# Cross-attention kernel: x scaled in turned form from group 2 on, constant products in the ramp, gain of two groups on VectorE

## The reference

```
# layer 0, once for s = a (ctx_512) and once for s = v (fside)
x1n = ln(x) * g1_s + b1_s ; x2n = ln(s) * g2_s + b2_s
q, k, v = x1n @ Wq_s + bq_s, x2n @ Wk_s + bk_s, x2n @ Wv_s + bv_s
out_s = softmax(q @ k.T * E**-0.5) @ v @ Wo_s + bo_s
res = out_a + out_v + x
y = (ln(res) * g + b) @ fc_W + fc_b + res
# layer 1
Q, K, V = y @ Wq + bq, ctx_512 @ Wk + bk, ctx_512 @ Wv + bv
result = y + softmax(Q @ K.T * E**-0.5) @ V @ Wo + bo
```

## Time and profile before

| | us |
|---|---|
| median of 3 executions | 154.44 |
| lowest and highest | 153.74 and 155.4 |
| the profiled execution, its time | 154.15 |
| the profiled execution, span of its instructions | 152.1 |
| TensorE busy | 144.1, 95% of the span |
| VectorE busy | 119.7, 79% |
| ScalarE busy | 117.0, 77% |
| GpSimd busy | 83.7, 55% |

### The profile page before, as it was taken

How to read it: one execution, slowest core, us unless ns; L and a number is a source line. 1 busy time by engine, 2 the same in 40 slices (tenths; PEclk the granted TensorE clock), 3 DMA queues, 4 the chain that set the end, 5 groups by cost and what they waited for, 6 DMA issues and landing times.

```text
span 152.1 us, 6148 instructions
## 1 busy us (share of the span) xinstructions
PE 144.1 (95%) x2320; PEld 104.1 (68%) x2320; DVE 119.7 (79%) x351; ACT 117.0 (77%) x410; POOL 83.7 (55%) x112
## 2 busy tenths in 40 slices
PE   5999999799999999999999999999999999999771
PEld 5987767688566766656866767657874877766440
DVE  1557999968899979899889757988677799668733
ACT  3436778568989788967977999787996878796970
POOL 2566999679438861878177575595674141201220
PEclk9999999999999999999999999999999999999998
DMA  5995799570770608786445019707300402201215
GB/s 154 346 386 179 227 312 370 142 274 3 238 241 15 211 8 263 237 232 186 165 144 173 4 43 244 248 8 249 135 4 0 142 2 73 73 0 69 75 71 207
DMA packets 13449, 23.40 MB, mean 154 GB/s; under 512 B 1660, under 2 KB 4332, under 8 KB 13420
## 3 DMA queue, kind: packets, MB, share of 16 engines
q1 hardware_dynamic: 12988, 22.61, 45.6%
q10 hardware_dynamic: 432, 0.41, 0.8%
HBM read 18.69 MB, written 4.32 MB: 151 GB/s over the span
## 4 chain that ended last, share of the span: by engine, by line
PE 92%; ACT 3%; issue 2%; DVE 1%; POOL 0%; POOLq 0%; ACTq 0%
PE ps L1758 10%; PE ps L1740 10%; PE ps L1699 9%; PE ps L1773 6%; PE ps L1731 6%; PE ps L1709 6%; PE ps L1747 6%; PE ps L1766 5%; PE ps L1574 5%; PE ps L1808 5%; PE ps L1684 5%; PE ps L1719 5%; PE ps L1783 4%; PE ps L1800 3%; PE ps L1791 2%
## 5 line engine op out<-in xcount | busy, mean ns | idle before, releaser
L579 POOL TENSOR_TENSOR prob<-exp,rsum 128x512 f32<-128x512 f32 x16 | 16.7, 1044 | 23.6 <-DVE rsum L1231 23.4
L585 POOL TENSOR_TENSOR prob<-exp,rsum 128x256 f32<-128x256 f32 x16 | 9.8, 616 | 19.7 <-DVE rsum L1300 19.6
L539 POOL TENSOR_TENSOR cfv_sb<-cf_sb,rows 128x512 f32<-128x512 f32 x16 | 17.0, 1061 | 5.8 <-PE ps L1731 3.5
L844 ACT ACTIVATE exp<-ps,exp_bias 128x64 f32<-128x64 f32 x64 | 19.3, 322 | 1.0 <-DVE exp_bias L1295 0.9
L825 ACT ACTIVATE gain_sb<-ps,res_rstd 128x128 f32<-128x128 f32 x64 | 18.3, 372 | 1.6 <-PE ps L1758 1.2
L547 POOL TENSOR_TENSOR cfk_sb<-cfv_sb,rows 128x512 f32<-128x512 f32 x16 | 17.0, 1060 | 1.1 <-POOL rows L532 0.2
L1758 PEld LDWEIGHTS ps<-wd,resT_sb 128*128 128x128 f32 x128 | 15.8, 191 | 2.3 <-issue 1.9
L1758 PE MATMUL ps<-wd,resT_sb 128*128 128x130 f32 x128 | 17.3, 278 | 0.0
L1699 PE MATMUL ps<-zT_sb,m 128*128 128x512 f32 x32 | 17.0, 617 | 0.0
L1740 PE MATMUL ps<-mix_sb,w 128*128 128x512 f32 x32 | 16.8, 608 | 0.0
L555 POOL TENSOR_TENSOR zT_sb<-xt_sb,x_spread 128x512 f32<-128x512 f32 x12 | 15.2, 1278 | 2.7 <-DMA x_spread<-rows_dram 2.4
(11 more groups left out here) (148 smaller groups left out, 342.5 us busy)
## 6 DMA issues: line engine op xcount, KB each, us to landing
x_sb<-in_x SPq DMA_DIRECT2D x16, 256.0 KB, 3.8
xt_sb<-in_xt SPq DMA_DIRECT2D x16, 256.0 KB, 3.9
out<-out_sb SPq DMA_DIRECT2D x16, 256.0 KB, 2.2
cf_sb<-in_cf SPq DMA_DIRECT2D x15, 256.0 KB, 3.3
x_spread<-rows_dram SPq DMA_DIRECT2D x6, 512.0 KB, 4.7
ct_sb<-in_ct SPq DMA_DIRECT2D x16, 128.0 KB, 4.0
w_sb<-in_w SPq DMA_DIRECT2D x1, 448.0 KB, 4.5
cf_sb<-in_cf ACTq DMA_DIRECT2D x1, 256.0 KB, 4.5
```

The lines of the kernel that those rows point to most:

```text
L539: pool.tensor_tensor(cfv_sb[:, g % CFV_SLOTS, :, :, :], cf_sb[:, g % CF_SLOTS, :, :, :], wide_cf(cf_rstd, g), ALU.mult).then_inc(cfv_pool, 1)
L579: pool.tensor_tensor(prob0[:, g % PROB0_SLOTS, :, :, :], exp0[:, g % EXP0_SLOTS, :, :, :], wide0(rsum0, g), ALU.mult).then_inc(prob0_done, 1)
L844: last = nc.scalar.activation(exp1[:, g % EXP1_SLOTS, p, :], ps[:, bank + u, v * S:(v + 1) * S], ACT.Exp, bias=exp1_bias[:, g, p:p + 1], a ...
```

## The change

The groups that are scaled and then transposed are 0 and 1 in place of 0 to 3, and the way over DRAM begins with batch 2. The gain of groups 14 and 15 goes to VectorE (`early_gain`, which was there but unused), and the probabilities of group 15 in layer 1 are formed by VectorE (`late_probs1`). TensorE's first run of constant products has 6 in place of 13, one more follows between `fold_v` and `fold_a`, and eight stand in the ramp behind the folds, before `t0(0)`, `s0(0)`, `s0(1)` and `out0(0)`. The order on all five queues is written anew. The core of the diff:

```diff
-TURNED = [0, 1, 2, 3]
+TURNED = [0, 1]
-SPREAD_FROM = 3
+SPREAD_FROM = 2
-GAIN_ON_DVE = []
+GAIN_ON_DVE = [14, 15]
+PROB1_ON_DVE = [15]
...
+        def prob1_ready(eng, g):
+            ready(eng, g, PROB1_ON_DVE, prob1_dve, prob1_pool)
...
             load_x(0)
+            load_wk()
+            load_w128()
+            load_wt()
+            load_wv()
+            load_x(1)
             load_cf(1)
-            load_wk()
-            load_wv()
-            load_w128()
-            load_x(1)
+            load_x(2)
             load_cf(2)
             load_cf(3)
...
             load_cf(7)
-            load_xt(0)
+            store_rows(2)
+            load_xt(1)
+            load_cf(8)
             load_x(6)
-            load_xt(1)
             load_xt(2)
+            spread_x(2)
...
+            scale_cf(1)
             z(1)
-            scale_cf(1)
             shifts(1)
+            shifts(2)
             shift_cf(1)
-            z(2)
-            z(3)
             scale_cf(2)
-            shifts(2)
+            shift_cf(2)
             probs0(0)
-            shift_cf(2)
+            shifts(3)
             scale_cf(3)
+            probs0(1)
+            scale_cf(4)
+            scale_xt(2)
+            scale_xt(3)
             shift_cf(3)
...
+            def late_probs1(g):
+                dve.wait_ge(rsum1_done, g + 1)
+                need(dve, prob1T_made, g - PROB1_SLOTS + 1)
+                v.tensor_tensor(prob1[:, g % PROB1_SLOTS, :, :], exp1[:, g % EXP1_SLOTS, :, :],
+                                wide1(rsum1, g), ALU.mult).then_inc(prob1_dve, 1)
...
             pe.wait_ge(constants_made, 1)
-            keep_busy(13, 0)
+            keep_busy(6, 0)
             fold_v(0)
+            keep_busy(1, 6)
             fold_a(6)
-            keep_busy(3, 2)
-            zT(0, 2)
-            fold_bias(3)
-            keep_busy(1, 0, (wq_v_done, 1), (wk_v_done, 1))
+            fold_bias(2)
+            fold_am(3)
+            zT(0, 4)
+            fold_wv(5)
             fold_m0(0)
-            fold_wv(7)
+            keep_busy(1, 0, (m0_done, 1))
             t0(0, 0)
...
+            fold_fca(1)
+            cfT(0, 3)
+            keep_busy(3, 3, (cfT_copied, 1))
+            s0(0, 3)
+            fold_wfc(0)
+            zT(1, 7)
+            turn_rows(2, 1)
+            fold_w(0, (wfc_done, 1))
+            cfT(1, 1, (rowsT_copied, 1))
+            t0(1, 7)
+            keep_busy(3, 6, (t0_copied, 2))
+            s0(1, 6)
+            prob0T(0, 1)
+            fold_bq1(0, (out0_bias_done, 1))
+            cfT(2, 2)
+            mix0(0, 3)
+            turn_rows(3, 1)
+            keep_busy(1, 0, (bq1_done, 1))
+            out0(0, 0)
+            fold_t1b(7)
+            prob0T(1, 6)
+            resN(0, 0)
+            dense(0, 1, (cfT_copied, 3))
+            mix0(1, 3)
+            t0(2, 0, (res_stats_done, 1))
+            out0(1, 3)
+            x1T(0, 4)
+            t0(3, 7, (t1_bias_done, 1))
...
+            dense(14, 2, (bias_row_done, 14))
+            dense(15, 6, (x1T_done, 14), (mix1_copied, 12))
+            t1(13, 0, (exp1_done, 13))
+            x1T(14, 1)
+            prob1T(12, 2, (bias_row_done, 15))
+            s1(13, 3)
+            out1(11, 5, (bias_row_done, 16))
             t1(14, 0)
+            x1T(15, 7)
+            mix1(12, 1)
+            s1(14, 5, (final_done, 12))
+            t1(15, 7)
+            out1(12, 0)
+            s1(15, 2)
             prob1T(13, 4)
```

More of the change, by code:

```diff
@@ L1853, in _ @@
+            cfT(3, 7)
+            cfT(4, 1, (diff0_done, 3))
+            x1T(1, 2)
+            t0(4, 7, (cfT_copied, 4))
+            s0(3, 3, (bias_row_done, 2))
+            t1(1, 2)
+            cfT(5, 0, (rowsT_copied, 3))
+            prob1T(0, 7, (t0_copied, 5))
+            s1(1, 5)
+            s0(4, 3, (diff0_done, 4))
+            mix1(0, 1)
             prob0T(2, 7)
[L1854 to L1857 removed]
+            t0(5, 0, (cfT_copied, 6))
@@ new lines, in _ @@
+            x1T(2, 4, (res_stats_done, 4))
+            turn_rows(5, 7, (cfT_copied, 7))
+            prob0T(4, 6)
+            s0(6, 0, (bias_row_done, 3))
+            t1(2, 7, (rowsT_copied, 4))
+            prob0T(5, 4)
+            x1T(3, 5)
+            s1(2, 2, (bias_row_done, 4))
+            mix0(4, 6)
+            mix0(5, 0, (diff0_done, 7))
+            out1(1, 4, (x1T_done, 4))
+            out0(4, 6)
+            cfT(7, 0, (mix0_copied, 6))
+            t1(3, 1)
+            resN(4, 7)
@@ new lines, in _ @@
+            dense(4, 2, (exp1_done, 3))
+            out0(5, 0, (cfT_copied, 8))
+            t0(7, 1)
+            s1(3, 4, (final_done, 2))
+            x1T(4, 0, (res_done, 6))
+            prob0T(6, 6)
+            prob1T(2, 7)
+            resN(5, 1, (t0_copied, 8))
+            s0(7, 2, (bias_row_done, 5))
+            mix1(2, 6)
+            t1(4, 0)
+            t0(8, 1, (res_stats_done, 6))
+            s1(4, 6)
+            out1(2, 4)
+            mix0(6, 2, (diff0_done, 8))
+            dense(5, 0, (t0_copied, 9))
@@ new lines, in _ @@
+            cfT(8, 2, (mix0_copied, 7))
+            out0(6, 3)
+            cfT(9, 4, (final_done, 3))
+            t0(9, 5)
+            prob0T(7, 2, (cfT_copied, 9))
+            x1T(5, 0, (bias_row_done, 6))
+            resN(6, 7, (exp1_done, 5))
+            prob1T(3, 1)
+            s0(8, 2, (prob0T_copied, 8))
+            t1(5, 0)
+            mix1(3, 6, (res_stats_done, 7))
+            mix0(7, 4)
+            s1(5, 0)
+            s0(9, 2, (diff0_done, 9))
+            turn_rows(6, 7, (mix1_copied, 4))
@@ new lines, in _ @@
+            x1T(7, 1)
+            mix0(8, 2)
+            s1(6, 4)
+            out1(5, 6, (prob0T_copied, 10))
+            t1(7, 0)
+            out0(8, 1)
+            mix0(9, 2)
+            s1(7, 6, (final_done, 6))
+            t0(10, 0)
+            prob1T(6, 5)
+            turn_rows(7, 2, (mix0_copied, 10))
+            out0(9, 3)
+            resN(8, 0, (t0_copied, 11))
+            mix1(6, 1, (rowsT_copied, 6))
+            s0(10, 4)
+            out1(6, 6)
+            dense(8, 0, (res_stats_done, 9))
@@ new lines, in _ @@
+            out0(10, 5)
+            t0(12, 2, (rowsT_copied, 7))
+            prob0T(11, 3, (mix1_copied, 8))
+            dense(10, 0, (exp1_done, 9))
+            cfT(13, 2, (t0_copied, 13))
+            resN(10, 7)
+            mix0(11, 3)
+            s0(12, 5)
+            t0(13, 7, (res_stats_done, 11))
+            prob1T(8, 2, (cfT_copied, 14))
+            out0(11, 3)
+            cfT(14, 4)
+            s1(9, 0, (bias_row_done, 11))
+            mix1(8, 6, (t0_copied, 14))
+            out1(7, 2, (res_done, 12))
@@ new lines, in _ @@
+            s0(13, 4, (cfT_copied, 15))
+            dense(11, 6, (mix1_copied, 9))
+            x1T(10, 3, (final_done, 8))
+            t0(14, 2)
+            resN(11, 0, (exp1_done, 10))
+            prob0T(12, 1)
+            t1(10, 5, (diff0_done, 14))
+            s0(14, 2)
+            mix0(12, 0, (res_stats_done, 12))
+            cfT(15, 4)
+            t0(15, 5, (t1_copied, 11))
+            out1(8, 2, (diff0_done, 15))
+            prob0T(13, 0, (mix0_copied, 13))
+            x1T(11, 1)
```

1228 lines of the change are left out of this document (540 added, 688 removed).

## The result

| | median us | lowest to highest | runs |
|---|---|---|---|
| before | 154.09 | 153.29 to 155.4 | 4 |
| changed | 162.56 | 162.04 to 163.13 | 4 |

The ratio is 1.054 [1.046, 1.063]: the changed kernel is slower by 5.4%, and its time lies 5.6 us above the upper end of the range. The profiled execution took 162.04 us with a span of 160.2, 8.1 us more than before. The ratios of this document leave out executions that were over 1.5% longer than the fastest of their kernel, the medians do not, so that a median need not match its ratio.

The account below looks back on a forecast made before the run. TensorE's own work bounds the middle, a chain of short steps the tail; the change acts in ramp and tail. Terms -2.1, +0.4, +1.2, -0.9, waits 1.0 give -0.4; tail +0.1; total -0.3: median 154.1 us, eight-in-ten range 151.8 to 157.0.

Parts of the forecast that it names:

- the low clock: Ramp: TensorE's gap before fold_v may delay the clock's rise, at latest to t0(0); +0.4 us, bounds 0 and 0.75.
- Rival 2: Ramp: TensorE stays at the lower clock past t0(0), rising only behind s0(1); 157.3 us, chance 0.17.
- the likeliest case: Whole kernel: the prediction's own sum of terms, median 154.1 us, chance 0.48.
- Start of the folds: Ramp: shorter first run and earlier wk load let fold_v start at 5.15 in place of 7.24; -2.1 us.
- Constant products: Ramp behind fold_v: nine constant products in place of five, most on TensorE's path; +1.2 us.
- Transposes of x: Ramp: TensorE drops zT(2) and zT(3) for one more turn_rows; -0.9 us.
- New waits: Ramp: only two groups can start early, so TensorE has less to do while their chains run; 1.0 us.
- The hand trace: Ramp: new lists followed with late clock; s0(1) at 19.9, t0(2) at 27.3, out0(1) ends at 29.0.
- The path of x over DRAM: Ramp: rows of batch 2 land at 23.7, scale_xt(2) starts at 25.9; cost 0, 2.2 us to spare.
- Rival 3: Ramp: x_spread(2) lands late behind four loads, beyond the 2.2 us of cover; 156.4 us, chance 0.05.
- The tail: Last groups: gain and probabilities on VectorE save, out1(12) ahead of s1(15) costs 0.5; sum +0.1 us.
- Rival 1: Ramp: clock rises as early as before and the 1.0 us of waits are absent; 152.3 us, chance 0.30.

Follow-up runs that it names:

- a9: Changed kernel with 9 constant products in the first run in place of 6; 160.67 us, ratio 1.045 against the kernel before.
- b6: Kernel before with its first run of constant products cut from 13 to 6; 156.99 us, ratio 1.023 against the kernel before.
- a13: Changed kernel with its first run of constant products set back from 6 to 13; 156.0 us, ratio 1.016 against the kernel before.
- a13no8: Changed kernel with 13 products in the first run and without the eight in the ramp; 155.77 us, ratio 1.017 against the kernel before.
- a6no8: Changed kernel, still 6 products in the first run, without the eight in the ramp; 162.34 us, ratio 1.050 against the kernel before.
- bno5: Kernel before without the five constant products that stand behind the first 13; 151.32 us, ratio 0.982 against the kernel before.
- bno5p: bno5 with the layer 1 probabilities of group 15 on VectorE; 151.56 us, ratio 0.980 against the kernel before.
- an8z2: a13no8 with groups 2 and 3 scaled on GpSimd (early) and transposed on TensorE again; 159.13 us, ratio 1.016 against the kernel before.
- an8out1: a13no8 with s1(15) issued ahead of out1(12); 157.21 us, ratio 1.016 against the kernel before.
- an8tail: a13no8 with the gain of groups 14, 15 back on ScalarE and group 15's probabilities on GpSimd; 156.63 us, ratio 1.019 against the kernel before.

## Why the prediction was wrong

The failing step is **the low clock**, a term of +0.4 us with bounds of 0 and 0.75, and in two ways.

The first is when the clock rises. I let it rise by `t0(0)` at the latest and gave a later rise 0.17. It rose at about 22.4 us. Against a late rise I had written that from 5.15 to about 10 the engine has no long gap. This is true of the changed kernel (there is no wait between 5.51 and 14.1) and it did not help. Nor is an early rise enough: `a9` had the clock and lost it at the folds at about 9.4 us, `b6` had it at 6.26 and lost it at about 7.8. How much the length of the first run is worth, the ratios of `a13` and `b6` say: 3.8 and 2.3 points. Why the clock stays up or not over these folds is not shown.

The second is the price. The bound of 0.75 doubled only the matmuls of the folds, `zT(0)`, `fold_wv` and `fold_m0`, and not their latencies. The run that tells is `a13no8`, the changed list with the clock up. Its timeline of TensorE:

```profile
1.52 5.37 PE L1585 MATMUL ps<-ones,ident 128*128 128x128 f32 x26 [1.52 <-POOL ident L503]
6.73 0.39 PE L1588 MATMUL ps<-affine_v,wq_sb 128*128 128x129 f32 x2
...
9.36 0.61 PE L1688 MATMUL ps<-ident,z_sb 128*128 128x128 f32 x4
...
11.96 1.10 PE L1710 MATMUL ps<-zT_sb,m 128*128 128x512 f32 x2 [0.48 <-ACT m L715]
...
14.43 0.70 PE L1720 MATMUL ps<-cfT_sb,t_sb 64*64 64x64 f32 x32 [0.77 <-ACT cfT_sb L789]
...
19.62 0.69 PE L1720 MATMUL ps<-cfT_sb,t_sb 64*64 64x64 f32 x32 [0.87 <-ACT t_sb L794]
...
21.11 0.35 PE L1676 MATMUL ps<-biases,w_sb 128*128 128x1 f32 x2 [0.21 <-DVE out_bias L1156]
...
23.48 1.13 PE L1751 MATMUL ps<-mix_sb,w 128*128 128x512 f32 x2 [0.55 <-ACT mix_sb L820]
...
27.62 1.13 PE L1710 MATMUL ps<-zT_sb,m 128*128 128x512 f32 x2
28.59 1.02 PE L1751 MATMUL ps<-mix_sb,w 128*128 128x512 f32 x2
```

| stretch on TensorE | changed | `a13no8` | difference | `a6no8` |
|---|---|---|---|---|
| to `fold_v` | 5.51 | 6.73 | -1.22 | 5.69 |
| `fold_v` to `t0(0)` | 9.61 | 5.23 | +4.38 | 9.01 |
| `t0(0)` to `s0(0)` | 5.34 | 2.47 | +2.87 | 3.99 |
| `s0(0)` to `s0(1)` | 6.82 | 5.19 | +1.63 | 8.77 |
| `s0(1)` to `out0(1)` | 8.48 | 8.97 | -0.49 | 10.01 |
| `out0(1)` to the end | 124.4 | 124.7 | -0.3 | 125.1 |

The whole loss is in the second to fourth stretch, 8.9 us, with 1.2 given back by the earlier start and 0.8 behind `s0(1)`: 6.9 us of span, of which the ramp has all. The two kernels differ in the eight products too. In the changed kernel one of them stands in the second stretch and three each in the third and fourth, 0.59, 1.58 and 0.86 us from start to start, together 3.0 of the 8.9. `a6no8` has neither them nor the clock, and its column gives the low level alone, for as long as it lasted in that execution. Ahead of `t0(0)`, where my bound allowed 0.75, it costs 3.78 us (9.01 against 5.23): the folds stand one behind the other on TensorE, and the small ones, down to those of one column, grew nearly as much as the large (two pairs of one column from start to start 0.24 us in `a13no8`, 0.44 in the changed kernel). Without the wait of 0.48 us for `m`, which both have, the stretch is 1.8 times as long. Rival 2 had the mechanism right and the place nearly (a rise behind `s0(1)`; in the changed kernel it came between `s0(0)` and `s0(1)`), but took over this price for the folds and counted 3.2 us behind them, from `t0(0)` to `s0(1)`. There the changed kernel has 4.5 more than `a13no8`, and `a6no8`, where the clock did come up only behind `s0(1)`, has 5.1 more without a single product. So the likeliest case and the rival erred by the same row. By the rule that I quoted from the Trainium skill (TensorE: Matmul & The Clock Gate, What's actually happening) the sum was to take the later bound or more: the trace agrees with the more.

The other steps:

- **Start of the folds.** Forecast 5.15, measured 5.51 (-1.73 in place of -2.1); `fold_v` waited 1.06 us for `affine_v`. Right in kind, 0.4 off. The six products ended at 4.45, forecast 4.2, which cost nothing here.
- **Constant products.** +1.2 for four more. At either level of the clock the eight weigh nothing that can be told (0.1 and 0.4 points, where their forecast length of 2.1 us would be 1.4). That a product on TensorE's path costs its length held for the five in the profiles of `bno5` and `bno5p`, not for the eight. In `a13no8` TensorE waits ahead of `t0(0)`, `s0(0)` and `s0(1)`, the places where they stood, so I take them to have filled waiting time there.
- **Transposes of x.** -0.9. Not seen: `an8z2`, which takes them back, has the ratio of `a13no8`. But 0.9 us is 0.6 points, less than these intervals can tell.
- **New waits.** +1.0 was too small. In `a13no8` the waits for `m`, `cfT_sb`, `t_sb`, `out_bias` and `mix_sb` are 0.48, 0.77, 0.87, 0.21 and 0.55, 2.9 us, where TensorE had hardly waited before: from 10 to 26 us it was busy 15.81 us before and is 12.92 in `a13no8`. The first three, 2.1 us, stand ahead of `s0(1)`. With the order of the work they use up the 0.9 of the transposes, the 1.0 of four products fewer than before and the 0.5 of the earlier `fold_v`: `s0(1)` comes at 19.62, before at 19.61. The hand trace put `t0(2)` at 27.3 with a late clock and the eight products; `a13no8` gets there at 27.62 with neither, though its folds start 1.6 us later than I had let them. So it was too kind by 0.3 + 0.75 + 2.1 - 1.6, an estimate of about 1.5 us, with the late clock at the 0.75 that the hand trace had in it. I lay the waits to the two chains in flight in place of four, which I had named and priced at a third; no run brings the two chains back, so this is argued and not shown.
- **The path of x over DRAM.** Right in the changed kernel and in `a13no8`, with little to spare. In the changed kernel the spread was issued at 26.05 (forecast 19.0) and `scale_xt(2)` began at 33.18 without waiting; in `a13no8` it began at 26.00, forecast 25.9. Rival 3 did not occur in either. With the clock up its mechanism is real all the same: the landings that I took as 4.7 us are up to 6.9, and in the profile of `an8out1` the cover was gone and `t0(2)` waited 1.07 us.
- **The middle.** Right: as many matmuls in 80 us as before, and `a13no8`, even with the kernel before at `s0(1)`, is still even at the start of `dense(15)` (137.28 and 137.40).
- **The tail.** +0.1. From the start of `dense(15)` to the end of the span it is 14.7 us before (137.40 to 152.1) and 16.0 in `a13no8` (137.28 to 153.3). The part behind `s1(15)` is 9.45 and 9.34, as forecast; the 1.4 us stand ahead of it, 6.68 us from the start of `dense(15)` to `s1(15)` (forecast about 6.5), before 5.25. TensorE has one wait of 0.22 in it, so the new list has more work there. I had booked this work as moved from elsewhere; the profile of `a13no8` is 1.2 us longer than that of before, though even with it at `s0(1)` and at `dense(15)`, so the tail is where those profiles part. Neither `an8tail` nor `an8out1` changed the time by more than the noise.

Rival 1 did not happen even with the clock up: 1.017, where it asked for 0.986.

In sum, the forecast of 154.1 was 8.5 us short. About 5.9 of them (3.8 points) go with the length of the first run, and about 2.5 remain with 13 products (1.6 points), where the waits and the tail were priced too low.

**What stays open** is the composition of the 1.6 to 1.7 points that remain with 13 products first. The profile of `a13no8` shows 1.2 us of span, and it was the shortest of that kernel's four executions. The order of `out1(12)`, the tail's engines, the eight products and the DRAM way were each undone with no difference that the ratios can tell, which leaves room for several tenths of a point in each; the loads may hold 0.7. A list that brings back two more early chains as a whole was not tried.

## What to carry to other kernels

Work that nobody reads can be the most valuable in a ramp: before shortening it, see by the length of like instructions where the clock rises, and price a late rise as nearly the doubling of everything on TensorE's path (here 1.8 times), small matmuls included, until a row shows the short form again. Then look at which of the filler is needed: here thirteen products in place of six at the start are worth 2 to 4 per cent, and taking out the five behind them gave nearly 2, of which the profiles explain about 0.7.

Read the beginning of the clock's row with suspicion, since both levels look the same in it until the first rise.

## What the runs showed of the hardware

The clock, once up, can fall while TensorE works without a wait. Busy by stretch in `a13`:

```profile
5.00:8.00 3.00, 3.00 (x16) 2.77 (x15) 0.04 (x1) 0.95 (x4) 1.06 (x2) 1.00 0.87 258
8.00:10.00 2.00, 2.00 (x16) 1.75 (x16) 1.75 (x8) 0.78 (x4) 0.20 (x1) 1.00 1.02 381
10.00:12.00 2.00, 2.00 (x14) 1.75 (x14) 1.66 (x9) 0.58 (x1) 1.83 (x4) 0.79 1.05 397
12.00:15.00 3.00, 2.61 (x14) 1.89 (x14) 2.60 (x12) 1.19 (x6) 1.54 (x3) 0.50 0.98 361
```

TensorE is busy 7.00 of 7.00 us from 5 to 12, and the granted clock goes from 1.00 to 0.50 within the third row. The matmuls of this stretch are folds, several with one column, and `zT(0)`. That their form brings the fall is not shown: in `a13no8` the clock stayed up over the same list. The Trainium skill (TensorE: Matmul & The Clock Gate, HAM oscillation) lays falls to waits of TensorE for data, of 3 to 5 us in its example; `b6` and `a9` had a shorter wait ahead of theirs (1.81 and 0.92 us), `a13` had none.

Where the first rise falls is not fixed by the list of TensorE. Alike down to the folds, the first run of 26 instructions took 5.92 us before, 5.69 in `bno5p` and 4.79 in `bno5`, and in the new order 5.92 in `a13` and 5.37 in `a13no8`. In the profile of `bno5` that moved `fold_v`, and all behind it, by about 1.1 us, which is a reason to want more than one profile of a ramp.
